# The f16 exponentials as a VectorE copy of the f32 ones instead of a second ScalarE exponential

## What is computed

```python
e = jax.nn.relu(_rho_signed_sqrt(q[:, :, None, :] + k[:, None, :, :]))
scores = jnp.einsum('bija,a->bij', e, Wphi)
m = jnp.max(scores, axis=-1, keepdims=True)
ex = jnp.exp(scores - m)
denom = jnp.sum(ex, axis=-1)
part1 = jnp.einsum('bij,bjc->bic', ex, Vy)
Ew = jnp.einsum('bij,bija->bia', ex, e)
part2 = jnp.einsum('bia,ca->bic', Ew, We_w) + We_b * denom[..., None]
return (part1 + part2) / (denom[..., None] + EPS_DEN)
```

## Time and profile before

| | us |
|---|---|
| median of 3 runs | 1383.87 |
| lowest, highest | 1381.85, 1384.41 |
| the profiled execution, its whole time | 1383.03 |
| the profiled execution, its span | 1381.3 |
| busy in the span: PE, DVE, ACT, POOL | 1210.2, 1212.5, 1135.1, 888.8 |
| a steady block, from one `split` to the next | 30.05 |

### The profile page before, as it was taken

The page is one execution under the profiler, slowest core; times in us unless marked ns, Lnnn a source line. Parts: engine busy times, 40 slices in busy tenths (PEclk is TensorE's granted clock), DMA queues, the critical chain, the costliest instruction groups (busy, mean ns, idle before and its releaser), DMA issues.

```text
span 1381.3 us, 21175 instructions
## 1 busy us (share of the span) xinstructions
PE 1210.2 (88%) x6185; PEld 575.5 (42%) x6185; DVE 1212.5 (88%) x3409; ACT 1135.1 (82%) x1292; POOL 888.8 (64%) x1294
## 2 busy tenths in 40 slices
PE   3899999998659999888999989899988889998886
PEld 2577667676422333333333333333333333333333
DVE  5777989896778899999999999989999998999997
ACT  1776888886369998999999899999989999998950
POOL 0764733332007888888888788888888888888820
PEclk9999999999769999999999999999999999999998
DMA  6001100000000001000000100000000000001001
GB/s 193 9 11 24 30 1 0 0 1 1 20 0 16 20 20 28 23 27 20 20 20 20 32 23 24 20 20 20 20 31 27 20 21 20 20 21 31 28 20 35
DMA packets 38843, 32.36 MB, mean 23 GB/s; under 512 B 6150, under 2 KB 35609, under 8 KB 38738
## 3 DMA queue, kind: packets, MB, share of 16 engines
q1 hardware_dynamic: 37714, 29.76, 7.4%
q0 software_dynamic: 1024, 1.35, 0.6%
HBM read 29.10 MB, written 2.75 MB: 23 GB/s over the span
## 4 chain that ended last, share of the span: by engine, by line
DVE 35%; PE 32%; issue 5%; ACT 1%; POOL 0%; POOLq 0%; DVEq 0%; ACTq 0%
DVE arena L1051 21%; PE ps L1331 10%; PE ps L1344 9%; DVE arena L1037 5%; PE ps L1388 4%; PE ps L1408 4%; DVE s L1083 3%; DVE x L1094 2%; PE ps L1380 2%; PE ps L1362 2%; DVE spread L1103 2%; DVE nmax L1043 1%; PE ps L1366 1%; ACT arena L1190 1%; DVE shift L1045 0%
## 5 line engine op out<-in xcount | busy, mean ns | idle before, releaser
L1051 DVE SCALAR_TENSOR_TENSOR arena<-arena,ps 128x512 f32<-128x512 f32 x1024 | 663.8, 677 | 69.8 <-PE ps L1344 68.5
L1190 ACT ACTIVATE arena<-arena,eps 128x4096 f32<-128x4096 f32 x128 | 474.2, 3709 | 6.0 <-ACT arena L1178 5.7
L1308 POOL TENSOR_SCALAR arena<-kT,negq 128x512 f32<-128x512 f32 x480 | 344.0, 723 | 170.8 <-DVE arena L1051 161.8
L1344 PE MATMUL ps<-spread,sel 128*128 128x512 f16 x1024 | 357.9, 386 | 101.1 <-DVE arena L1051 95.0
L1314 POOL TENSOR_SCALAR arena<-arena,q 128x512 f32<-128x512 f32 x480 | 348.0, 735 | 22.4
L1344 PEld LDWEIGHTS ps<-spread,sel 128*128 128x128 f16 x1024 | 91.9, 97 | 491.5 <-DVE arena L1051 376.0
L1331 PE MATMUL ps<-arena,phi_cols 128*32 128x512 f32 x2048 | 276.3, 614 | 7.7 <-ACT arena L1190 7.7
L1178 ACT ACTIVATE arena<-kT,q 128x512 f32<-128x512 f32 x330 | 217.1, 712 | 44.3 <-DVE arena L1051 44.3
L462 POOL TENSOR_SCALAR kT<-kT,region 128x512 f32<-128x512 f32 x128 | 88.8, 694 | 155.6 <-DVE region L587 155.0
L512 ACT ACTIVATE kT<-ps,region 128x512 f32<-128x512 f32 x128 | 88.0, 687 | 59.4 <-DVE region L582 57.9
L1395 PE MATMUL ps<-z,wge 128*128 128x512 f32 x256 | 130.8, 593 | 0.3 <-DVE z L1077 0.3
(11 more groups left out here) (196 smaller groups left out, 1714.9 us busy)
## 6 DMA issues: line engine op xcount, KB each, us to landing
wge<-in_e_wg SPq DMA_DIRECT2D x32, 256.0 KB, 2.7
w1e<-in_e_w SPq DMA_DIRECT2D x32, 128.0 KB, 2.1
w2e<-in_e_w SPq DMA_DIRECT2D x32, 128.0 KB, 2.1
w3e<-in_e_w SPq DMA_DIRECT2D x32, 128.0 KB, 2.1
region<-in_w SPq DMA_DIRECT2D x1, 2048.0 KB
out<-x SPq DMA_DIRECT2D x4, 256.0 KB, 2.8
region<-in_wqk SPq DMA_DIRECT2D x1, 512.0 KB, 4.7
region<-in_wv SPq DMA_DIRECT2D x1, 512.0 KB, 5.4
```

Of the source, the lines that this page charges most:

```text
L1051: dve.scalar_tensor_tensor(feat[:, j, k, :], feat[:, j, k, :], 1.0, psB[:, k % BANKS, :], ALU.mult, ALU.mult, accum_out=sums[:, j, gg, c:c ...
L1190: act.activation(grp, grp, ACT.Sqrt, bias=eps[:]).then_inc(e_ready, 2)
L1308: pool.tensor_scalar(feat[:, j, QUADS * gg + c, :], kT[:, b * N:(b + 1) * N], HUGE, negq[:, b % 2, at - b * N // 2:at - b * N // 2 + 1], A ...
L1344: pe.matmul(psB[:, k % BANKS, :], sel[:, gg, c, :], spread[:, j, :], start=True, stop=True).then_inc(bc_done, 1)
```

## The change

ScalarE's second exponential goes. `exh` is made by VectorE from `ex` with a copy that converts f32 to f16, at slot (6, 3) of the block before, ahead of the `split` at slot (7, 1) that reads it. `exh_ready` is now signalled by VectorE. The copy waits for `ex_ready` and for the block before's `split` (`spread_ready`). For the first block it stands right ahead of the first `split`. PE's next scores wait for `ex_ready` where they waited for `exh_ready`.

```diff
-        SPLIT_AT, SILU_AT, LIFT_AT = (7, 1), ((7, 0), (7, 2)), 6
+        ROUND_AT, SPLIT_AT, SILU_AT, LIFT_AT = (6, 3), (7, 1), ((7, 0), (7, 2)), 6
...
+                def round_ex(m, j):
+
+                    dve.wait_ge(ex_ready, m + 1)
+                    if m:
+                        dve.wait_ge(spread_ready, m)
+                    dve.tensor_copy(exh[:], ex[:, j, :]).then_inc(exh_ready, 1)
...
+                            ROUND_AT: lambda: final or round_ex(m + 1, 1 - j),
                             SPLIT_AT: lambda: final or split(m + 1, 1 - j, before=1 if none else 2),
...
                 dve.wait_ge(b3_added, B)
+                round_ex(0, 0)
                 split(0, 0, before=0)
...
                     act.activation(ex[:, j, :], psS, ACT.Exp, bias=shift[:, j:j + 1]).then_inc(ex_ready, 1)
-                    if before:
-                        act.wait_ge(spread_ready, m)
-                    act.activation(exh[:], psS, ACT.Exp, bias=shift[:, j:j + 1]).then_inc(exh_ready, 1)
...
                     if gg == 0 and not first:
-                        pe.wait_ge(exh_ready, m)
+                        pe.wait_ge(ex_ready, m)
```

## The result

The changed kernel is slower, by less than forecast: 1391.97 us median of six runs against 1383.41 of the kernel before, a ratio of 1.0071 (95% interval 1.0051 to 1.009), so 9.8 us where 24.9 were predicted, and the median lies 2 us below the range. (The two medians themselves are 8.6 us apart; the ratio with its interval isn't theirs, and the runs of each kernel scatter over 5.5 to 6 us.) A second set of six runs on another occasion gave the same ratio, 1392.59 against 1384.59 us (1.0053 to 1.0089). Two later runs, one of 31 of the kernel before (1402.06 us, mean granted clock 0.93) and one of the kernel with the exponential left out (1989.4 us, 0.56), ran at a much lower clock than their like and are left out of the ratios.

What follows compares the result with a forecast made beforehand. Taken as bound: PE's full stretch, then VectorE's, in each 30.05 us block. 32 copies, 29 of them at 0.82 us, added 24.9 us to 1383.03; with the median 0.8 above, 1408.8 us, range 1394.0 to 1412.0.

Steps and rivals of the forecast that it cites:

- The bound: In each 30.05 us block PE is full for 13.11 us, then VectorE for 16.91 of 16.94 us; nobody waits for ScalarE.
- The removal costs and gives nothing: ScalarE's 0.57 us per second exponential end in a wait for PE's product ahead of the second tanh: worth nothing.
- The bare copy, 0.35 us: An unhindered copy on VectorE takes 0.43 us, less 0.08 us overlap with the next instruction: 0.35 us, the low end.
- rival (b): Conversion to 16 bits halves the copy's rate on VectorE: a step of 0.61 us, 19.5 us in all, 1403.4; chance 0.08.
- The meeting with GpSimd: At 862.77 us GpSimd leads the copy by 0.06 to 0.07 us and wins: copy 0.90 us, a step of 0.82.
- the sum: 29 steady copies at 0.82 us, two at 0.35 (blocks 0 and 30), one at 0.43 ahead of the blocks: 24.9 us.
- Rival (a): VectorE gets the port first, or the wait counts only in part: 11.3 us added, 1395.2 us; chance 0.16.
- The range: From 1394.0 to 1412.0 us, the upper end for a further remainder of 0.1 us in each block.
- What is late next: Sums, SiLU products and `split` queue behind the copy, so its whole step passes through; `split` isn't held up by GpSimd.
- Rival (e), the ports even out: VectorE comes first at 851.38 and at the copy: 11.9 us come back for 11.3 added, 1383.3 us; chance 0.04.

Runs made afterwards that it cites:

- the moved kernel: The kernel before with VectorE's features of group 2 made by ScalarE instead: 1361.23 us, ratio 0.9853, blocks of 29.33 us.

## Why the prediction was wrong, step by step

- **The bound.** Right. Two stretches, each full of one engine; shown by the extra copy in either one (0.34 and 0.03 us a block).
- **The removal costs and gives nothing.** Right, with its reason: the wait ahead of the second tanh took all of it, in the changed kernel (20.5 us), and in the one with the exponential left out (21.2 us).
- **The bare copy, 0.35 us.** Right: 0.34 us. The conversion to f16 costs nothing extra (0.42 us where the f32 copy takes 0.43), rival (b) is out. What the prediction set beside it was read in part: the section of the Trainium skill that it cites, "The TRN2 errata" of "VectorE: DVE Perf Modes", says itself that its table's 58 cycles are too few for one operation and gives about 150 as measured, from which I estimate (150 + 256) / 0.96 = 423 ns, and with that the trace agrees (416 ns).
- **The meeting with GpSimd.** Its time, place and lead came out as forecast in all 29 blocks. *"I take it that GpSimd wins"* is the step that failed. It put 0.82 us in the sum where 0.34 were right, and 29 times 0.48 = 13.9 us is nearly the whole miss of 24.9 - 9.8 = 15.1. The rule before it, that who starts first has the port, failed in the same place: GpSimd started first in all 29 blocks, and the copy was not held up. The rows that I took it from had a per-partition operand, L1037 in the earlier trace rows and `split` in the earlier trace rows, and "lead, length and kind are those of the earlier trace rows" left this operand out. Rival (a) named what came, a shorter copy that may ask for the port at another moment, and got 0.16. With such an operand the kernel takes 1409.09 us and its blocks 30.89, so the rest of the sum stands.
- **The range.** With (a) at 1395.2 and a low end of 1394.0 I gave that case no room below it. The copies sum to 31 x 0.34 + 0.45 = 11.0 us by the trace, and the ratio's interval, 7.1 to 12.5 us, holds that; the median fell 2.4 us lower. Of the runs one can't say where. In the two profiles, the first `split` comes 2.4 us earlier in the changed kernel although a copy stands ahead of it (the first row of small matmuls, above, 3.0 us), and between the first and the last `split` 8.7 us are added instead of 10.5. Of that difference 0.8 us are two longer blocks in the profile of before, the one of the earlier trace rows among them, 0.4 us one shorter block in that of after, and 0.5 us the first block, which is 0.14 us shorter instead of 0.34 longer. A range built on one profiled execution has to allow for such things even where the steady block is known to a hundredth.
- **What is late next.** Right for the copy as it came out: `split` keeps its 0.74 us. For a copy that loses it was nearly right: with the operand `split` takes 0.75 to 0.76 us in nearly all blocks.
- **Rival (e), the ports even out.** Not seen: the feature instruction's 0.90 us stayed in the steady blocks. That its removal pays was seen in the moved kernel.

## What to carry to other kernels

Find the stretch in which an engine is full before pricing an instruction on it: one and the same copy cost 0.34 us a block in VectorE's stretch and next to nothing in TensorE's, and ScalarE, busy 93% of the block, could be relieved without any gain and be loaded without any loss. Where two engines share a port and start within a tenth of a microsecond of each other, a row from another form of instruction doesn't say who wins; give both outcomes their full weight, and where the values allow it try a bare copy or a constant in the instruction instead of an operand read per partition. An instruction that pays for the port in every block is a good first candidate to move to another engine.

## What the runs showed of the hardware

Who has the shared port is not decided by the starts in the trace. Behind a feature instruction of GpSimd's that starts 0.067 us earlier, a bare copy and a multiplication with a constant in the instruction are not held up (0.42 us), and one with an operand read per partition is (0.90 us). Against the same kind of GpSimd instruction, started after a wait, a bare copy won with a lead of 87 or 88 ns against it and lost with 89 to 92, at the one place where this was seen; against GpSimd's lift, whose constants stand in the instruction, it already loses with 48 to 58 ns, and in the one such meeting with a lift that reads an operand per partition it lost with 68. What sets GpSimd's side stays open. The Trainium skill's rule that whoever issues first holds the pair and the other fully blocks ("SBUF — State Buffer", section "Who interferes with whom") agrees with the runs in its second half: a loser on VectorE ended a fixed time after GpSimd's instruction, whether that had 0.31 or 0.66 us left. Its first half can't be read off the starts that the profile shows.

The loser's price is regular. A copy or a TENSOR_SCALAR of this size on VectorE that loses ends 0.28 us after GpSimd's instruction (0.62 + 0.28 = 0.90 for the copy with an operand at slot (6, 3), 0.54 + 0.28 = 0.82 for the bare one at slot (6, 1), 0.39 + 0.28 = 0.67 for the extra one at slot (0, 3)). `split` ends 0.54 us after it (0.31 + 0.54 = 0.85 with the copy at slot (6, 1), 0.66 + 0.54 = 1.20 in the earlier trace rows). So a short remainder is free: with the 0.20 us that `split` had in the kernel before, 0.20 + 0.54 comes to its usual 0.74.
